# Band addition, temperature and row maximum of the logits in one two-input VectorE operation

## What is computed

```python
x = _layernorm(h)                                    # (256, 512)
key = jnp.einsum('bsd,de->bse', x, K)
logits = jnp.tanh(jnp.einsum('bsd,btd->bst', key, x) + bias[0])
band = (lower[:, None] <= idx[None, :]) & (idx[None, :] < upper[:, None])
logits = logits - 10000.0 * (1.0 - band.astype(logits.dtype))
logits = logits * temperature
scores = jax.nn.softmax(logits, axis=-1)
h = h + jnp.einsum('bst,btd->bsd', scores, x)
```

## Time and profile before

| what | value |
|---|---|
| time, median of 3 runs | 1676.42 us (1675.86 to 1678.04) |
| span of the profiled execution, first to last instruction | 1665.0 us |
| median less span | 11.4 us |
| busy: TensorE | 1474.2 us (89%) |
| busy: VectorE | 1170.4 us (70%) |
| busy: ScalarE | 646.5 us (39%) |
| busy: GpSimd | 607.2 us (36%) |
| GpSimd's addition L730, 64 instructions | 84.6 us |

### The profile page before, as it was taken

How to read it: one execution, slowest core, us unless ns; L and a number is a source line. 1 busy time by engine, 2 the same in 40 slices (tenths; PEclk the granted TensorE clock), 3 DMA queues, 4 the chain that set the end, 5 groups by cost and what they waited for, 6 DMA issues and landing times. The chain is left out here.

```text
span 1665.0 us, 32506 instructions
## 1 busy us (share of the span) xinstructions
PE 1474.2 (89%) x9853; PEld 1312.3 (79%) x9853; DVE 1170.4 (70%) x2638; ACT 646.5 (39%) x1297; POOL 607.2 (36%) x1598
## 2 busy tenths in 40 slices
PE   3677877759999999999999999999999937999994
PEld 3566666649999999999999999999999935665652
DVE  1422222237988988998999998988988836778772
ACT  1221211214554545455445544454544423333330
POOL 2000000002555555555555555555565550101111
PEclk9799989979999999999999999999999967999997
DMA  9999999941112121212221122112121110000000
GB/s 372 423 428 429 429 427 428 405 128 51 67 65 78 65 77 64 77 64 71 69 76 64 64 76 72 68 64 76 66 74 40 40 39 9 8 6 2 7 3 3
DMA packets 58603, 211.15 MB, mean 127 GB/s; under 512 B 9524, under 2 KB 12160, under 8 KB 46016
## 3 DMA queue, kind: packets, MB, share of 16 engines
q1 hardware_dynamic: 47216, 172.85, 26.6%
q10 hardware_dynamic: 5200, 33.62, 5.0%
q0 software_dynamic: 6144, 4.14, 0.9%
HBM read 139.28 MB, written 73.07 MB: 128 GB/s over the span
## 5 line engine op out<-in xcount | busy, mean ns | idle before, releaser
L185 PE MATMUL s1b<-pg,cg 128*128 128x256 f32 x1024 | 246.3, 402 | 95.3 <-DVE cg L136 89.7
L185 PEld LDWEIGHTS s1b<-pg,cg 128*128 128x128 f32 x1024 | 204.6, 202 | 136.6 <-ACT stage L211 46.2
L418 PE MATMUL ps_kx<-xThi,Khi 128*128 128x256 f32 x1024 | 288.9, 282 | 3.6 <-DVE xTlo L670 3.5
L420 PE MATMUL ps_kx<-xThi,Klo 128*128 128x256 f32 x1024 | 288.6, 282 | 0.0
L419 PE MATMUL ps_kx<-xTlo,Khi 128*128 128x256 f32 x1024 | 288.5, 282 | 0.0
L136 DVE TENSOR_TENSOR cg<-xg,se 128x2048 f32<-128x2048 f32 x32 | 73.3, 2292 | 231.2 <-DMA pg<-in_pct_dram 209.5
L418 PEld LDWEIGHTS ps_kx<-xThi,Khi 128*128 128x128 f32 x1024 | 197.5, 193 | 4.2 <-DVE xTlo L670 4.2
L419 PEld LDWEIGHTS ps_kx<-xTlo,Khi 128*128 128x128 f32 x1024 | 193.2, 189 | 0.0
L420 PEld LDWEIGHTS ps_kx<-xThi,Klo 128*128 128x128 f32 x1024 | 193.1, 189 | 0.0
L577 ACT ACTIVATE o<-h,sh,sc 128x512 f32<-128x512 f32 x128 | 97.4, 808 | 233.3 <-POOL sh L807 233.3
L211 ACT COPY stage<-s1b 128x512 f32<-128x512 f32 x128 | 65.7, 600 | 259.0 <-PE s1b L185 252.6
(11 more groups left out here) (126 smaller groups left out, 3435.7 us busy)
## 6 DMA issues: line engine op xcount, KB each, us to landing
pg<-in_pct_dram SPq DMA_DIRECT2D x32, 2048.0 KB, 27.7
xg<-in_xs_dram SPq DMA_DIRECT2D x32, 1024.0 KB, 22.9
spec<-stage ACTq DMA_DIRECT2D x64, 512.0 KB, 8.5
xt<-spec SPq DMA_DIRECT2D x64, 512.0 KB, 3.6
out_dram<-o SPq DMA_DIRECT2D x64, 512.0 KB, 2.8
recs<-rec POOLq DMA_DIRECT2D x16, 160.0 KB, 16.9
recs<-rec,idx POOLq DMA_INDIRECT x128, 3.1
Wf<-in_Wm_dram SPq DMA_DIRECT2D x1, 1520.0 KB, 27.9
```

The lines of the kernel that those rows point to most:

```text
L185: last = nc.tensor.matmul(bank[(b % 2) * 4 + m // 2][:, m % 2, :], cg[:, b % 2, m * 2 + h, :], pg[:, b, m * 2 + h, :], start=(h == 0), sto ...
L418: nc.tensor.matmul(out_ap, whi, mhi, start=(j == 0), stop=False)
L420: last = nc.tensor.matmul(out_ap, wlo, mhi, start=False, stop=(j == n - 1))
```

## The change

The tanh is no longer followed by GpSimd. VectorE waits for the tanh itself (and for the exponentials of the image before, which read `lg`), executes an empty instruction, and makes two passes that each read `th` and `band`, write (th + band) x temperature into `lg` and give the maximum of what was written, starting from the lowest float32, to `mx`. GpSimd's addition and its semaphore `pool_l` are gone. ScalarE's next tanh, which overwrites `th`, waits for VectorE's second pass instead of GpSimd's addition. The new operation is one of the VectorE operations with a program of their own, loaded with the kernel, and not of the built-in ones.

```diff
--- before.py
+++ after.py
@@ -35,6 +35,7 @@
 WCOLS = 3 * P + 224
 TJ = 8
 MAGIC = 12582912.0
+LOWEST = -3.4028235e38
 
 
 def wait(eng, sem, value):
@@ -347,7 +348,6 @@
         dve_wb = sem("dve_wb")
         dve_v4 = sem("dve_v4")
 
-        pool_l = sem("pool_l")
         pool_nmx = sem("pool_nmx")
         pool_ve = sem("pool_ve")
         pool_rstd1 = sem("pool_rstd1")
@@ -520,7 +520,7 @@
                 if has(i - 1):
 
                     act.wait_ge(pe_logit, i)
-                    wait(act, pool_l, i - 1)
+                    wait(act, dve_max, (i - 1) * 2)
                     nc.scalar.activation(th[:, :, :], ps_l[:, :, :], ACT.Tanh,
                                          bias=bias[:, 0:1]).then_inc(act_tanh, 1)
 
@@ -585,11 +585,14 @@
             def slot(i, k, has):
                 if has(i - 1):
 
-                    dve.wait_ge(pool_l, i)
+                    dve.wait_ge(act_tanh, i)
+                    wait(dve, act_exp, (i - 1) * 2)
                     wait(dve, pool_nmx, i - 1)
-                    for t in range(TILES):
-                        nc.vector.tensor_scalar(lg[:, t, :], lg[:, t, :], temp[:, 0:1], None, ALU.mult,
-                                                ALU.max, accum_out=mx[:, t:t + 1]).then_inc(dve_max, 1)
+                    settled(dve)
+                    for t in range(TILES):
+                        nc.vector.tensor_tensor_reduce(out=lg[:, t, :], in0=th[:, t, :], in1=band[:, t, :],
+                                                       scale=temp[:, 0:1], scalar=LOWEST, op0=ALU.add, op1=ALU.max,
+                                                       accum_out=mx[:, t:t + 1]).then_inc(dve_max, 1)
                 if has(i - 2):
 
                     n, r4, r2 = i - 2, (k + 2) % 4, k % 2
@@ -723,11 +726,6 @@
         @block.gpsimd
         def _(pool):
             def slot(i, k, has):
-                if has(i - 1):
-
-                    pool.wait_ge(act_tanh, i)
-                    wait(pool, act_exp, (i - 1) * 2)
-                    nc.gpsimd.tensor_tensor(lg[:, :, :], th[:, :, :], band[:, :, :], ALU.add).then_inc(pool_l, 1)
                 if has(i + 1):
                     n, r4 = i + 1, (k + 1) % 4
                     pool.wait_ge(dve_mv1, n * 2 + 2)
```

## The result

The changed kernel takes 1704.78 us (1703.10 to 1706.36, 4 runs) against 1676.28 us of the kernel before: ratio 1.0168, 95% interval 1.0153 to 1.0182. It is slower by 28.5 us where 2.0 us less was forecast, and outside the range. The profiled execution has a span of 1704.6 us and a time of 1706.36 us, so 1.8 us lie around the span.

What follows compares the result with a forecast made beforehand. TensorE alone was taken to bound the second stage's loop, so gains came only at its edges: 0.6 + 0.15 + 1.25 = 2.0 us, from 1676.42 to 1674.4 us. The range was 1672.4 to 1677.2 us.

Steps and rivals of the forecast that it cites:

- The waits: VectorE's, ScalarE's and GpSimd's changed waits in each slot: next to no cost, the empty instruction 0.05 us, only on the drain.
- rival (b): Nothing moves: GpSimd's 2.06 us stall shifts to where it hurts, or slow pass and clock cancel; about 1676.4 us, chance 0.13.
- long done: VectorE's added wait for the exponentials of the image before, claimed to be already satisfied when VectorE reaches it.
- The stall at slot 60: First slots after the loop: removing the addition absorbs the lateness from GpSimd's 2.06 us stall in slot 59; gain 0.6 us.
- Slot 63: The same TensorE wait for the mask, smaller, in slot 63: 0.27 us against 0.12, gain 0.15 us.
- The drain: Single chain from the last tanh to the stage's end, shortened up to the negated maximum: gain 1.25 us (0.71 to 1.38).
- The first image: First image, where VectorE and GpSimd operations collide: gain 0 to 0.3 us, taken as 0.
- rival (a): The clock adds to the gain, returning earlier in the drain and last stage: 4.0 us gain, 1672.4 us, chance 0.2.
- The new pass: VectorE's two-input pass with maximum, 256 elements: 412 to 747 ns, taken as 477, the old pass's time.
- The time around the span: 11.4 us between the profiled span of 1665.0 us and the time of 1676.42 us, claimed to stay unchanged.
- (c): VectorE becomes the bound, at 1.5 us a pass in some 60 slots: +24 us, about 1698 us, chance 0.03.
- (d): The new pass is split, with the maximum in another full sweep: 1675.0 us, counted in the forecast's case, no separate chance.

Runs made afterwards that it cites:

- the run at before's length: The changed kernel without VectorE's wait for the exponentials, list 1317 instructions: 1663.39 us, ratio 0.9983 to the kernel before.
- the repeat of the changed kernel: The changed kernel with 112 empty instructions that the compiler dropped, so unchanged, on another chip: 1697.08 us, ratio 1.0187 to the kernel before.
- the run with the waits alone: The kernel before, addition and old pass kept, with the change's waits and empty instruction ahead of the VectorE pass: 1698.6 us, ratio 1.0191.
- the one with 16 fills behind all tensors: The kernel before with 16 one-column fills behind VectorE's second stage, into a tensor allocated last so no other moves: 1699.8 us, ratio 1.0186.
- 24 fills: The changed kernel with 24 one-column fills behind VectorE's second stage, into a tensor allocated last: 1664.16 us, ratio 0.9984 to the kernel before.
- the run with 16 dropped empty instructions: The kernel before with 16 empty instructions behind VectorE's second stage, which the compiler dropped: 1666.73 us, ratio 1.0001.
- N = 8: The kernel before with 8 one-column fills behind VectorE's second stage, into a tensor that moves the stage's others: 1699.54 us, ratio 1.0192.
- N = 9, 16: The kernel before with 9 or 16 such one-column fills, into a tensor that moves the others: 1703.74 us (ratio 1.0221) and 1703.26 us (1.0218).

## Why the prediction was wrong

**What bounds the kernel now.** Right for the second stage: TensorE's slot is 15.220 us in both kernels, no wait in the loop. Its gap was the last stage. I read its first 15 us for the clock, and not its end, where the answer to "which engine ends the span, and which would if it were later" stands. VectorE's branches end at 1650.0 of 1665.0 us there: 15.0 us of cover, less than the 44.5 us that the same branches gained.

**The failed step.** It is "The waits": "The empty instruction costs nothing to 0.1 us". As time in the slot that holds (482 ns a pass, no wait in the loop). As places in VectorE's list it does not: 16 written-out slots, one instruction more in each, move the loop behind them by 16, over the edge of a piece. There was no term in the sum for the fetching of instructions, on any engine whose list the change makes longer. I had such a thought once, in rival (b), and for the wrong engine: GpSimd's code becomes shorter, and its stall might move. It did not move: the 2.06 us stand at the same transfer in the changed kernel (1279.77). That the change alters VectorE's list by the same count, and that behind it stands a loop with eleven empty steps, I did not ask. The wait that I called "long done" is what made most of the list's growth, 14 of the 16 places: without it the kernel gains (the run at before's length).

**The size of it.** On the chips of the experiments, the shift costs 32.5 us by the kernel before (1699.8 - 1667.3), and 33.7 by the changed one (1697.08 - 1663.39). In the changed kernel's profile 44.5 - 14.7 = 29.8 us of it is the empty steps. The other 9.7 us are the later last dest: 10.4 lost in the five steps with work, where packets come too (1600.9, 1603.8, 1606.2, 1608.6), less the 0.8 that it was ahead before them. There dest comes every 51.0, 50.9, 51.0, 49.8 us before, and every 52.8, 52.6, 56.5, 51.4 us after. The 56.5 holds one wait of TensorE of 5.7 us, behind ScalarE standing still for 8.0 us, released by nothing on this core:

```profile
ACT act_hi L992 <- remote: 13.2, 2, 8.0
```

Neither the repeat of the changed kernel nor the run with the waits alone nor the one with 16 fills behind all tensors has that row; there the same stretch, from count_i to the last dest, is 1.6 to 2.5 us longer than before. So about 2 us of the 10.4 come with the place of the loop in every run, and the rest is this execution's or its chip's own; the kernels' times on one chip differ by 28.5 us, the two profiles by 39.5. What ScalarE waited for stays open.

**The terms of the sum, each.** The stall at slot 60: the slot that lasted 15.92 us lasts 15.22, gain 0.70, summed 0.6; the mask product follows the last key product by 1288.45 - 1288.33 = 0.12 us. Slot 63: 1332.67 - 1332.56 = 0.11 for 0.27, gain 0.16, summed 0.15. The drain: from tanh to the negated maximum 1344.52 - 1342.60 = 1.92 us against 1345.16 - 1342.06 = 3.10, gain 1.18, summed 1.25. Together 2.0 us, as forecast. The first image, taken at 0 with 0.3 us allowed, gave a little besides: its softmax slot lasts 14.74 us against 14.98, in the repeat and with 24 fills too, and 14.93 at before's length. Over the whole stretch from slot 59's first key product to count_i it is 104.22 us against 105.98, 1.8 us less. Only 0.8 of it is in hand at count_i, since this execution came to slot 59 0.99 us later (1267.57 against 1266.58), 0.66 of them already at the first key product of the second stage. The run at before's length shows 3.0 (1.2 to 4.3), and its interval takes in both the forecast and rival (a).

**The new pass.** 482 ns, 1% over what I took. The Trainium skill's rule, in "Vector Engine (DVE) Microarchitecture Reference", section "Points that are easy to get wrong", on two SBUF sources would have put it at the slow end; no run here shows that loss for this operation. The exclusive lock of the Trainium skill, "SBUF — State Buffer", section "SBUF: two separate sides", does show, on GpSimd: its two-column ve lasts 1269 ns on average (218 in the earlier trace rows), now that it no longer stands behind the tanh and starts together with VectorE's xnlo, which has two SBUF inputs, and ends just behind it, in 52 of 53 slots:

```profile
886.97 1.22 DVE L712 TENSOR_TENSOR xnlo<-xn,xnhi 128x1024 fp32r<-128x1024 f32 x1
886.97 1.29 POOL L733 TENSOR_SCALAR ve<-mv 128x2 f32<-128x2 f32 x1 [1.47 <-DVE mv L699]
```

GpSimd is 35% busy, and TensorE does not wait for it inside the loop.

**The time around the span.** "11.4 us lie around it and stay" was no measured thing. Every execution whose time and span both are given, of this kernel and of before, has 1.8 to 2.0 us around it. The 11.4 came from setting one execution's span of 1665.0 us beside the median of others. Before takes 1676.3 us on one chip and 1666.4 to 1667.3 on two others, and the span with 1.9 us around it would be 1666.9: the two numbers did not belong together. It moves no term of the sum, but the profile of before seems to come from one of the faster chips, and that makes the spans' difference (39.5 us) larger than the times' (28.5 us).

**The rivals.** (a) can't be told from the forecast by the time of the run at before's length. Its trace shows the premise and not the price: half clock in the drain lasts 6.8 us there instead of 10.2, and full clock is back at 1388.4 us, 3.5 us earlier than in the kernel before, though the last stage begins only 1.9 to 2.2 us earlier. But from count_i to the last dest it gained 0.4 us (271.95 against 272.33 in the run with 16 dropped empty instructions, on the same chip), where (a) had priced 1.7. (b) and (c) fell: nothing moved to TensorE, and VectorE did not become the bound. (c) had a time of the right sort for the wrong reason. (d) fell: one pass of 482 ns. The chance of 0.07 for slower was made of (c) and the first stage; the mechanism that decided had none.

## What to carry to other kernels

Count what an edit does to the length of each engine's instruction list, waits and empty instructions too, and ask which loops stand behind it on that engine: in this kernel a loop of 288 instructions is cheap at one place and costs 33 us more sixteen places on, and the profile's rows for instruction queues, 21 packets against 56, are the sign. Where a kernel gets slower with no busy engine at its end, look at the branches and at what ends the span; and where a small edit gives a result out of proportion to its size, shift the code and the tensors each by themselves, unrelated work, before explaining the edit. The runs with fills in a tensor that moved the others show why both must be held still.

## What was not expected of the hardware

- An empty turn of a loop costs VectorE 1.04 us or 9.53 us, by the place of the loop in the list (start 984 or 1000). A jump with two instruction packets behind it takes 3.4 to 3.8 us, with one 2.3 to 2.7 us, with none 0.32 to 0.38 us.
- TensorE's key product of 256 columns starts every 117.8 ns, or every 113.3 ns when the stage's tensors stand 128 bytes further on; with 32 bytes (N = 8) it is 118.3 and with 64 (N = 9, 16) 120.0 ns. The 128 bytes are worth 11.8 us here, six times the change's own gain.
- The pass with two SBUF inputs, a scale and a running maximum lasts as long as the one with one input: 482 and 477 ns for 256 elements.
- A two-column operation of GpSimd lasts 0.22 us, or 1.27 us when it starts with VectorE's two-input xnlo of 1.22 us.
